# Message layers: a table of blocks and slots per lot of seven items, read with a fourteen-number register load, in place of a packed path word per two lots

## The reference, cut to what matters

```
h = relu(layernorm(x));  msg = relu([h[src], h[dst]] @ W_msg + b)      # layer 0
x = x + relu([h, segment_sum(msg, dst) / max(count, 1)] @ W_upd + b)
h = relu(layernorm(x));  msg = h[src] * norm                           # layer 1
x = x + (segment_sum(msg, dst) + h) @ W.T + b
x = x + attention layer (edges, softmax per target)                    # layer 2
x = x + expm-like Taylor diffusion over the edges, 4 x 20 terms        # layer 3
```

## Time and profile before

| | us |
|---|---|
| median of 3 timed runs | 5065.65 |
| span of the profiled execution (first to last instruction; no other time is known of it) | 5595.3 |
| `plan_items` | about 42 to 77 |
| `edge_sums`, layer 0 | 746.7 to about 1403 |
| `edge_sums`, layer 1 | 1755.9 to about 2322 |
| one lot of PE where it waits for no messages | about 4.4 |

### The profile page before, as it was taken

One profiled execution on the slowest core, in us unless ns is written; L12 is line 12 of the kernel. 1 busy time (PEld: TensorE's weight loads), 2 busy tenths in 40 slices (PEclk: granted clock), 3 DMA queues, 4 the chain that ended last, 5 costly groups with the idle time before them and its releaser, 6 DMA issues. The chain is left out here.

```text
span 5595.3 us, 57187 instructions
## 1 busy us (share of the span) xinstructions
PE 3211.8 (57%) x11864; PEld 1985.9 (35%) x11864; DVE 2682.7 (48%) x6366; ACT 1037.9 (19%) x1952; POOL 2831.6 (51%) x2538
## 2 busy tenths in 40 slices
PE   3554726555895268775666626777735545455534
PEld 1222515444674157552222214555522222222212
DVE  6877722111453022364666625777754444444423
ACT  0222411111221011121211102333311111111100
POOL 0364048886113850134666646777515555587741
PEclk7776655555555555555555555555557777776665
DMA  5222621111562110253111132443311111133214
GB/s 186 83 60 69 263 91 22 22 22 17 141 162 80 23 16 1 73 198 111 36 35 36 35 55 47 79 95 69 79 54 29 28 28 28 27 31 28 28 16 95
DMA packets 337013, 363.38 MB, mean 65 GB/s; under 512 B 236964, under 2 KB 268846, under 8 KB 336864
## 3 DMA queue, kind: packets, MB, share of 16 engines
q1 hardware_dynamic: 222752, 262.44, 14.4%
q0 software_dynamic: 94096, 80.75, 11.4%
q10 hardware_dynamic: 20016, 18.41, 1.0%
HBM read 188.07 MB, written 188.35 MB: 67 GB/s over the span
## 5 line engine op out<-in xcount | busy, mean ns | idle before, releaser
L843 PE MATMUL e_ps<-e_msg,e_hot 128*128 x2408 | 583.2, 424 | 540.0 <-issue 304.5
L843 PEld LDWEIGHTS e_ps<-e_msg,e_hot 128*128 128x128 f32 x2408 | 538.0, 327 | 631.3 <-issue 627.1
L1733 POOL DMA_INDIRECT u_a<-attended,dst_end x392 | 468.5, 1195 | 153.4 <-issue 115.5
L815 DVE TENSOR_TENSOR e_ps<-e_ps,e_before 128x65 f32<-128x65 f32 (+1 forms) x172 | 40.1, 233 | 991.9 <-PE e_ps L843 513.6
L2364 PE MATMUL d_pl<-d_hot,d_fields 128*65 128x512 f32 x712 | 498.2, 866 | 0.0
L2019 POOL DMA_INDIRECT list<-s_rec,s_place x200 | 201.5, 1008 | 316.6 <-DVE s_place L1935 258.0
L735 POOL DMA_INDIRECT e_msg<-from_src,e_src x200 | 205.6, 1028 | 288.2 <-DMA e_first<-lot_first 233.8
L2308 POOL DMA_INDIRECT flows<-d_out,d_end x160 | 263.4, 1646 | 106.6 <-issue 101.7
L2295 POOL DMA_INDIRECT d_near<-term,d_rec x196 | 190.8, 973 | 236.4 <-DMA d_rec<-list 181.5
L938 POOL DMA_INDIRECT a_ends<-h,a_src x200 | 197.6, 988 | 202.9 <-DMA a_etype<-in_etype 113.8
L2356 PE MATMUL d_pr<-ident,d_scan 65*128 65x65 f32 x356 | 63.6, 327 | 400.8 <-DVE d_scan L2474 341.1
(11 more groups left out here) (369 smaller groups left out, 7774.3 us busy)
## 6 DMA issues: line engine op xcount, KB each, us to landing
u_z<-h SPq DMA_DIRECT2D x28, 896.0 KB
x<-sums SPq DMA_DIRECT2D x28, 896.0 KB, 7.8
u_x<-x SPq DMA_DIRECT2D x28, 896.0 KB
terms<-s_zeros SPq DMA_DIRECT2D x16, 812.5 KB
s_key_row<-src_key SPq DMA_DIRECT2D x50, 256.0 KB
h1d<-u_h SPq DMA_DIRECT2D x14, 910.0 KB
u_z<-h1d SPq DMA_DIRECT2D x14, 910.0 KB
term<-u_h SPq DMA_DIRECT2D x14, 910.0 KB
```

The costliest lines, as they stand in the source:

```text
L843: last = nc.tensor.matmul(to, hot[s][:, q, :], rows, start=False, stop=q == LOT - 1)
L1733: pool.indirect_dma_start(A[s][:, j, :], None, net.attended[:, :], bass.IndirectOffsetOnAxis(ap=net.dst_end[:, tile:tile + 1], axis=0)).th ...
```

## The change

`plan_items` writes a table of 16 words per lot: seven block numbers, seven slots (tile minus first tile of the lot, the same number as before), one word with the number of chunks to wait for (last block shifted right by 2, plus 1), one word unused. The thirteen shifts and thirteen ORs go. The table has 86 x 16 words, 5504 bytes, where the words before had 172 bytes. PE takes the fourteen numbers of a lot by one load instruction with fourteen registers, without a bounds check, and the fifteenth by a `value_load`; it does so in every lot, after the fifth matmul, for the lot that follows. The unpacking is gone, and so is the sum for the wait.

```diff
-        at = sb("at", [1, PAIRS, 2 * LOT], I32)
-        step = sb("step", [1, PAIRS, 2 * LOT], I32)
-        lots = sb("lots", [1, PAIRS], I32)
+        lots = sb("lots", [1, LOTS, LOT_WORDS], I32)
...
+                nc.vector.memset(lots[:, :, :], 0)
...
-                nc.vector.tensor_copy(at[:, :, :], block_of[0:1, 0:PAIRS * 2 * LOT].rearrange("o (g q) -> o g q", q=2 * LOT))
+                by_lot = block_of[0:1, 0:LOTS * LOT].rearrange("o (g q) -> o g q", q=LOT)
+                tiles_by_lot = tile_of[0:1, 0:LOTS * LOT].rearrange("o (g q) -> o g q", q=LOT)
+                nc.vector.tensor_copy(lots[:, :, 0:LOT], by_lot)
+                nc.vector.tensor_tensor(lots[:, :, LOT:2 * LOT], tiles_by_lot, tiles_by_lot[:, :, 0:1].to_broadcast([1, LOTS, LOT]), ALU.subtract)
                 nc.vector.tensor_copy(first_of[:, :], tile_of[0:1, 0:ITEMS:LOT])
                 v.drain()
-                nc.vector.tensor_tensor(step[:, :, 1:2 * LOT], at[:, :, 1:2 * LOT], at[:, :, 0:2 * LOT - 1], ALU.subtract)
-                nc.vector.tensor_copy(lots[:, :], at[:, :, 0])
-                v.drain()
-                for q in range(1, 2 * LOT):
-                    nc.vector.tensor_scalar(step[:, :, q], step[:, :, q], BLOCK_BITS + q - 1, None, ALU.logical_shift_left)
-                v.drain()
-                for q in range(1, 2 * LOT):
-                    last = nc.vector.tensor_tensor(lots[:, :], lots[:, :], step[:, :, q], ALU.bitwise_or)
-                    v.drain()
+                nc.vector.tensor_scalar(lots[:, :, 2 * LOT], lots[:, :, LOT - 1], 2, None, ALU.logical_shift_right)
+                v.drain()
+                nc.vector.tensor_scalar(lots[:, :, 2 * LOT], lots[:, :, 2 * LOT], 1, None, ALU.add)
+                v.drain()
...
-                def read_pair(pair):
-                    path = pe.value_load(plan[0:1, pair:pair + 1], min_val=0, max_val=(1 << BLOCK_BITS + 2 * LOT - 1) - 1)
-                    blocks = item_blocks(pe, path)
-                    return blocks[0:LOT], blocks[LOT:2 * LOT]
-                pair = read_pair(0)
+                def read_lot(g):
+                    at = g * LOT_WORDS
+                    _, items = nc.values_load_multi_w_load_instructions(
+                        plan[0:1, at:at + 2 * LOT], engines=[mybir.EngineType.PE], min_val=0, max_val=BLOCKS - 1,
+                        skip_runtime_bounds_check_because="block numbers are cut off at the last block and slots are distances within a lot")
+                    chunks = pe.value_load(plan[0:1, at + 2 * LOT:at + 2 * LOT + 1], min_val=1, max_val=CHUNKS)
+                    return items[0:LOT], [u.with_bounds(min_val=0, max_val=LOT - 1) for u in items[LOT:]], chunks
+                after = read_lot(0)
                 for g in range(LOTS):
                     s = g % 2
-                    blocks = pair[s]
-                    slots = [pe.snap((blocks[0] + q - b).with_bounds(min_val=0, max_val=LOT - 1)) for q, b in enumerate(blocks)]
+                    blocks, slots, chunks = after
                     pe.wait_ge(placed, g + 1)
...
-                    pe.wait_ge(msg_ready, (blocks[-1] >> 2) + 1)
+                    pe.wait_ge(msg_ready, chunks)
...
-                        if s == 1 and q == LOT - 2 and g + 1 < LOTS:
-                            pair = read_pair(g // 2 + 1)
+                        if q == LOT - 3 and g + 1 < LOTS:
+                            after = read_lot(g + 1)
```

More of the change, by code:

```diff
@@ L41 @@
 ITEMS = LOT * (LOTS + 1)
-BLOCK_BITS = 8
-PAIRS = LOTS // 2
+LOT_WORDS = 2 * LOT + 2
 PLACES = LOT * LOTS - BLOCKS + LOT
@@ L356, in _ @@
                 sp.dma_start(net.item_lane[:, :], lane_of[:, :]).then_inc(stored, 16)
-                sp.dma_start(net.lot_plan[:, :], lots[:, :]).then_inc(stored, 16)
+                sp.dma_start(net.lot_plan[:, :], lots[:, :, :].rearrange("o g w -> o (g w)")).then_inc(stored, 16)
                 sp.dma_start(net.lot_first[:, :], first_of[:, :]).then_inc(stored, 16)
@@ L667, in _ @@
                 step(None, at(0, LAST))
[L670 to L675, removed]
 def edge_sums(nc, net, layer, sums):
@@ L700, in edge_sums @@
         numbers = sb("numbers", [P, P])
-        plan = sb("plan", [1, PAIRS], I32)
+        plan = sb("plan", [1, LOTS * LOT_WORDS], I32)
         first = sb("first", [1, LOTS + 1], I32)
@@ L2596, in program @@
     net.item_lane = table("item_lane", P, ITEMS)
-    net.lot_plan = table("lot_plan", 1, PAIRS, I32)
+    net.lot_plan = table("lot_plan", 1, LOTS * LOT_WORDS, I32)
     net.lot_first = table("lot_first", 1, LOTS + 1, I32)
```

## The result

Before: 5067.18 us, median of four runs (5063.07 to 5076.49; the three of the table above and one more). After: 4987.2 us, median of four (4978.42 to 4987.95). The ratio is 0.983, 95% interval 0.9815 to 0.984: 80 us faster, where 170 us slower was forecast.

What follows compares the result with a forecast made beforehand. PE's sequencer was taken to bound layer 1's lots, POOL layer 0. Lots going from 4.39 to 6.28 us give 92 x 1.89 = +174, the plan -4.5: 5065.65 + 174 - 4.5 = 5235 us, range 5044 to 5290.

Steps and rivals of the forecast that it cites:

- The clock (0.5): Both message layers: PE's granted clock is 0.5, the 1.2 GHz level, in nearly every slice, and would not change.
- the undisturbed lots as the base: PE's lots: the 530 us stretching belongs to one profiled execution, so differences from 4.387 us lots are added to the timed median.
- the plan: DVE's table building before the layers: 5.0 us removed, 0.5 us added for the larger table, -4.5 us in all.
- one instruction for the fourteen registers: PE's load stays one instruction; the rival, a split into fourteen, would give 5610 us, chance 2 in 100.
- The load of fourteen registers comes, in the same place, when that lead is used up: PE after the fifth matmul: the load's time plus a 0.06 us gap is added in full, a lot takes 3.90 + X.
- X: Duration of PE's fourteen-register load: 0.30 + 13 x 0.16 = 2.38 us, one trip per register, chance 0.52.
- if PE has more queued at the load than the 0.14 suggests: Sign of error at PE's load: each further 0.1 us of queued cover would take 9 us off the forecast.
- The lead that the prediction measured: PE's queued matmuls while its sequencer is away: a burst of 3.20 instead of 3.06 us, so 0.14 a lot.
- The two register operations per item (0.143 and 0.042) stay as they are: PE's sequencer at each item: both operations remain and, with the two waits, fit beside the data path.
- the middle rival: PE's load: trips overlap, 0.01 to 0.12 us per register, X 0.4 to 1.9, change -13 to +125 us; chance 0.20.
- the one trip for all: Rival on PE's load: one SBUF trip for all fourteen registers, X 0.30 to 0.39, 5048 us; chance 0.22.
- POOL's 12.37 us a chunk in layer 0: unchanged: Layer 0: POOL sets the pace, allowing 7.19 us a lot, which hides PE's longer lots except the last seven.

Runs made afterwards that it cites:

- e2: Kernel after the change, with a second load of the same fourteen words in every lot (blocks from one load, slots from the other): 5109.8 us.
- e3: Kernel after the change, but loading only seven block numbers and subtracting the slots on PE as before: lot 4.27 us, total time not stated.
- e1: The kernel before the change, run again without any edit and with its own profile: profiled span 5062.8 us.
- e5: Kernel after the change, with one more clearing matmul in every lot: 5019.5 us, lot 4.03 us.
- e6: Kernel before the change, with one more clearing matmul in every lot: 5063.7 us, lot 4.39 us.
- e8: Kernel after the change, with DVE's one-hots of a lot in seven pieces of 128 columns instead of one of 896: 4966.4 us.
- e10: Kernel before the change, with DVE's one-hots of a lot in seven pieces of 128 columns instead of one of 896: 5045.2 us.
- e7: Kernel after the change, with all sixteen words of a lot in one load and no separate chunk number load: 5003.2 us.
- e11: Kernel after the change, run again without any edit: 4984.6 us, layer 0 of 614.1 us.

## Why the prediction was wrong

**What held.** The diagnosis: layer 1 before was set by PE's sequencer at 4.387 us a lot, the data path below it is 3.66. Both numbers stood in the prediction, and the second is the lot after to the hundredth. The clock (0.5), the undisturbed lots as the base, the plan (4.5 us expected, 4.1 measured; of that DVE's part 5.0 expected, 4.3 measured) and one instruction for the fourteen registers (172 loads, no split) held too.

**The step that failed** is "The load of fourteen registers comes, in the same place, when that lead is used up. So what it takes, X, and a gap are added in full". With the measured X = 1.337 that sum, 3.90 + X, still gives 5.24 us a lot and 5139 us in all. It was 3.66, and 4987. The prediction had named the sign: "if PE has more queued at the load than the 0.14 suggests". The burst of 3.06 us, where it expected 5.6, is that sign. So the wrong size of X is the smaller half of the miss; adding it was the larger.

The lead that the prediction measured, 0.5 us or so by the earlier trace rows (a sequencer away for 0.6 us, a burst longer by 0.14), is the lead of a program in which the sequencer is the slower of the two. There the queue before the data path runs near empty, whatever it could hold. It says nothing of how far the sequencer gets ahead once it is the faster one. After the change, around the load at 1899.7 us, by lines of the source in short windows:

```profile
L833 PEldq FUSED_REGOPS  x5: 74/74/74, 1899.0 to 1899.6; - x5
...
L815 PEldq TENSOR_LOAD <-e_plan x1: 1339/1339/1339, 1899.7 to 1899.7; - x1
...
L818 PEldq TENSOR_LOAD <-e_plan x1: 306/306/306, 1901.1 to 1901.1; - x1
...
L833 PEldq FUSED_REGOPS  x2: 74/74/74, 1901.8 to 1901.9; - x2
```

The five operations from 1899.0 on are those of the lot whose burst begins only at 1901.51. So when the load begins, PE still has the end of one burst before it (to 1901.0), the clearing matmul and ten matmuls of the next, up to 1901.51 + 3.06 x 10/14 = 1903.7: 4.0 us of work. The sequencer is back at item six at 1901.8. It could stay away for 1.9 us longer in that lot, though not in every one: e2 shows the steady allowance, 0.3 to 0.4.

What bounds a lot is thus the larger of two sums, not one sum. The data path's is 3.66. The sequencer's, from starts in the trace between 1898.8 and 1902.5: wait 0.15, five items 0.77, load with its gap 1.40, chunk number 0.65, two items 0.30: 3.3, and for the rest of the 3.66 it waits. What it waits for is the one-hots of its next lot, which DVE can only write when PE is done with the lot before the current one:

```profile
1901.35 1.09 DVE L797 TENSOR_TENSOR e_hot<-e_lane,e_numbers 128x896 f32<-128x896 f32 x1
...
L828 PEldq EVENT_SEMAPHORE  x2: 51/51/51, 1898.8 to 1902.5; - x2
```

DVE ends at 1902.44 and the sequencer goes on at 1902.48 (L828 is the step behind the two waits). So the two buffers of one-hots, and no queue, end its lead here, at about one lot. e2 says the same (4.7 - 1.34 - a gap of 0.06). Before, the sequencer's sum was the 4.39. The Trainium skill has a figure that should have been weighed here: "Advanced Engine Details and Errata", section "Engine Queue Depths", gives TensorE a queue of 64 instructions. The trace agrees as far as it goes: some 16 matmuls with their weight loads, 30-odd instructions, stand before PE at the load. No run fills the queue further, so none shows its end.

**Second, a saving was missed**: "The two register operations per item (0.143 and 0.042) stay as they are". They became one of 0.074. From start to start an item takes 0.15 us of the sequencer (the five above start within 0.6 us, four steps), where the prediction left 0.143 + 0.042 and a gap each, about 0.32. That is seven times 0.17, or 1.2 us a lot, nearly the price of the load. e3 puts it back and the lot goes to 4.27: 3.3 + 1.2 - 0.28 for the shorter load = 4.2. So the three errors weigh differently. Adding X turned the sign by itself (5.24). The missed saving by itself would have made the change worth about nothing (3.3 + 1.2 = 4.5, against 4.39). The wrong X of 2.38 by itself would still have left it a little faster (3.3 + 1.04 = 4.34).

**Third, X**, 2.38 expected. 1.337 lies inside the middle rival ("a short cost per register", 0.4 to 1.9) and by its sum would have given 5139. The price of 0.16 for each further register was wrong, and the one trip for all (0.30 to 0.39) as well.

**Fourth, layer 0.** "POOL's 12.37 us a chunk in layer 0: unchanged". It is (1286.3 - 735.3) / 49 = 11.24 after and 11.63 in e1 (741.9 to 1311.8), by POOL's first and last sum of nodes. The 12.37 belonged to that one execution; the 0.39 per chunk, 17 to 19 us in all, are what POOL's gathers lose less by DVE's one-hots (27.4 us in e1, 9.0 after). That a change on PE shifts when DVE's one-hots begin was in no part of the prediction.

With the right terms the sum is 92 x (3.66 - 4.387) = -67 for the lots, -4 for the plan and -17 for POOL in layer 0: -88, where the medians have -80 and the profiled spans -86.

## What to carry to other kernels

The time of a loop on PE is the larger of its data path's sum and its sequencer's; a lead that is read from a loop bound by the sequencer is not what the queue can hold, so work moved onto the sequencer costs nothing until its own sum passes the data path's, as long as what stands before PE lasts longer than one stay (here 4.0 us of it, for a stay of 2.0). To tell which sum bounds a loop, add a little work to the data path alone, as e5 and e6 do. Count the register operations at each matmul as closely as those in the block that is removed, since a value that comes finished out of a table saves there. And where one layer goes by another engine, look at which instructions of DVE that engine's gathers meet, and how early in them, before calling it unchanged.

## What was not expected of the hardware

**A register load's price is not linear in its registers.** From this kernel's SBUF table on PE, medians: one register 0.305 us, seven 1.056, fourteen 1.337, fifteen 1.577, sixteen 1.105. Fifteen, with four ones in binary, is the dearest and sixteen, with one, is cheap for its size. A start of 0.18, 0.2 for each one in the binary count and 0.04 per register would fit all five within 0.12; three numbers fitted to five counts don't prove it, and no run loads eight.
The Trainium skill, in "Runtime: NRT & Kernel Launch", section "Instruction fetch mechanics", has about 200 ns per register, said of loads from HBM. Here it is 0.07 (16) to 0.31 us (1), from SBUF.

**A gather issued by POOL waits for a DVE instruction with two SBUF inputs**: 0.95 us alone, 1.76 and 1.82 when it begins just after a one-hot of 1.08, and in general longer by the rest of the one-hot less 0.12. A share of bandwidth would not give that line. Shorter DVE instructions make the wait shorter, at more DVE time (e8 to e10).
The Trainium skill, "SBUF — State Buffer", section "Who interferes with whom", says that VectorE and GpSimd share a port pair under an exclusive lock, and that a VectorE instruction with two SBUF inputs contends with a GpSimd instruction that reads SBUF. The trace agrees: the wait lasts as long as the one-hot. Of `tensor_tensor` the page also infers that it does not hold up descriptor generation; these gathers were held up. They read their row numbers from SBUF, and whether it is that read or the generation that waits, no run here shows.

**What stays open.** Why POOL loses less by the one-hots after the change than before, and most in e2, e3 and e7: each kernel has its own phase between POOL and DVE, that is, its own point of a one-hot at which the gathers fall. In the one kernel that was profiled twice it was the same (e11), and I can't work it out from the code. In e2 much of the loss was the clip's (L742, 1385 ns mean for 859), in e7 the second gather's. Without the split, such a phase is worth up to 36 us, nearly half of the change.
